# A hybrid layer on one core: feed-forward weights rounded inside the linear attention, residual and second norm by token blocks across the stage border, and value products issued later

## What is computed

```python
x = x + linear_attention(layernorm(x))     # 32 heads of 64, decayed state, rmsnorm over 2048, sigmoid gate, out_w
x = x + ffn(layernorm(x))                  # 256 -> 768 -> 256, silu(gate) * up, all three weights rounded to fp8 e4m3fn
x = x + softmax_attention(layernorm(x))    # 2 x 1024 tokens, 16 heads of 16, rotary, causal
x = x + ffn(layernorm(x))                  # the same weights and scales again

def _quantized_matmul(x, w, scale):
    wq = w.astype(jnp.float8_e4m3fn).astype(x.dtype)
    return jnp.einsum('bsi,io->bso', x, wq) * scale
```

## Time and profile before

| | us |
|---|---|
| median of 3 runs (1264.12 to 1267.35) | 1265.59 |
| the profiled execution, its own time | 1261.26 |
| its span, first to last instruction | 1259.5 |
| PE busy (14272 products) | 1116.5, 89% |
| DVE busy | 636.3, 51% |
| ACT busy | 586.5, 47% |
| POOL busy | 483.2, 38% |

### The profile page before, as it was taken

One profiled execution on the slowest core, in us unless ns is written; L12 is line 12 of the kernel. 1 busy time (PEld: TensorE's weight loads), 2 busy tenths in 40 slices (PEclk: granted clock), 3 DMA queues, 4 the chain that ended last, 5 costly groups with the idle time before them and its releaser, 6 DMA issues. The chain is left out here.

```text
span 1259.5 us, 33418 instructions
## 1 busy us (share of the span) xinstructions
PE 1116.5 (89%) x14272; PEld 866.9 (69%) x14272; DVE 636.3 (51%) x1378; ACT 586.5 (47%) x1083; POOL 483.2 (38%) x507
## 2 busy tenths in 40 slices
PE   4999999999999999999954796884899999988698
PEld 3888988988888888889843675771344444435577
DVE  6234343343343343343456736885777777743742
ACT  3544344444444443443416542341466666675442
POOL 2355354445445454453522563204122222220255
PEclk9999999999999999999975898895999999999899
DMA  3101001010010100000030002155233333000001
GB/s 117 50 2 44 9 2 51 2 44 9 2 51 3 44 8 18 35 3 2 3 116 32 1 1 84 50 150 141 49 69 68 68 69 69 19 2 1 1 17 50
DMA packets 20809, 49.01 MB, mean 39 GB/s; under 512 B 2176, under 2 KB 11968, under 8 KB 17984
## 3 DMA queue, kind: packets, MB, share of 16 engines
q1 hardware_dynamic: 20672, 46.97, 13.2%
HBM read 34.18 MB, written 8.39 MB: 34 GB/s over the span
## 5 line engine op out<-in xcount | busy, mean ns | idle before, releaser
L1514 DVE TENSOR_REDUCE ca_mx<-ca_S 128x1 f32<-128x640 f32 (+1 forms) x192 | 176.7, 955 | 64.1 <-PE ca_S L1384 63.0
L1479 ACT ACTIVATE ca_PT<-ca_ST 128x512 f32<-128x512 f32 (+1 forms) x304 | 158.3, 579 | 90.1 <-PE ca_ST L1408 88.1
L499 PE MATMUL la_R<-a_hTh,la_Wh 128*128 128x512 f32 x384 | 154.1, 401 | 3.5 <-ACT la_k L294 3.5
L423 DVE SCALAR_TENSOR_TENSOR la_y<-la_g,la_O 128x512 f32<-128x512 f32 x64 | 41.1, 684 | 228.3 <-PE la_O L587 228.3
L499 PE MATMUL la_R<-a_hTl,la_Wh 128*128 128x512 f32 x384 | 150.6, 392 | 0.0
L499 PE MATMUL la_R<-a_hTh,la_Wl 128*128 128x512 f32 x384 | 150.2, 391 | 0.0
L1355 POOL TENSOR_SCALAR_AFFINE_SELECT ca_PT<-ca_PT 128x256 f32<-128x256 f32 (+1 forms) x112 | 48.9, 442 | 204.8 <-ACT ca_PT L1479 204.6
L430 DVE TENSOR_TENSOR X<-la_R,X 128x512 f32<-128x512 f32 x64 | 44.3, 692 | 147.3 <-PE la_R L499 147.3
L241 POOL TENSOR_TENSOR la_qd<-la_q,la_C 128x512 f32<-128x512 f32 x64 | 81.3, 1291 | 96.7 <-PE la_O L587 94.6
L253 POOL TENSOR_TENSOR la_yl<-la_y,la_yh 128x512 fp32r<-128x512 f32 x64 | 81.6, 1296 | 95.4 <-ACT la_yh L318 95.4
L233 POOL TENSOR_TENSOR la_Wl<-la_Wraw,la_Wh 128x512 fp32r<-128x512 f32 (+1 forms) x32 | 50.4, 1584 | 146.4 <-DVE la_Wh L446 114.1
(11 more groups left out here) (188 smaller groups left out, 2761.2 us busy)
## 6 DMA issues: line engine op xcount, KB each, us to landing
la_Wraw<-w_quads_dram SPq DMA_DIRECT2D x7, 1280.0 KB, 5.7
ca_VG<-V SPq DMA_DIRECT2D x8, 512.0 KB, 4.8
q_parts<-rp_QP SPq DMA_DIRECT2D x4, 768.0 KB, 3.7
k_parts<-rp_KP SPq DMA_DIRECT2D x4, 768.0 KB, 3.5
ca_KS<-k_parts SPq DMA_DIRECT2D x10, 256.0 KB, 7.2
qw_w<-w_ffn_dram SPq DMA_DIRECT2D x6, 384.0 KB, 5.2
X<-hidden_dram SPq DMA_DIRECT2D x4, 512.0 KB, 7.7
la_q<-hidden_dram SPq DMA_DIRECT2D x1, 2048.0 KB, 7.6
```

The costliest lines, as they stand in the source:

```text
L499: m = pe.matmul(out, a, b, start=n == 0, stop=n == len(pairs) - 1)
L1479: act.activation(PT[:, (NM2 * g + b) % NPT, h:h + nh, 0:w], ST[at % NB][:, 0:nh * w].rearrange("p (h q) -> p h q", h=nh), ACT.Exp, scale=S ...
L1514: dve.reduce_max(out, src, AXX).then_inc(s1_free, 1)
```

## The change

**The rounding** is a class now, `quantised_weights`, with twelve chunks of 128x384 and single buffers (two of `w`). Chunk c is done by the engines inside unit 16 + c of the linear attention, units 16 to 27; SP loads each chunk and stores the rounded one to DRAM (`q_ffn`), and gathers all of it into `WF` once slot 0 of the linear attention's weights, which now lies in `WF`, is free (unit 28). The queues run passes 0 and 1 as a loop and passes 2 and 3 written out.

**The border.** The sums of squares, roots, residual and norm go by token blocks (`last_sums`, `ln2`). Blocks 0 and 1 are summed after unit 29; in unit 30 ACT takes their root and DVE adds the residual of block 0 and takes its moments; in unit 31 DVE normalises block 0 and adds the residual of block 1, and PE turns block 0. The feed-forward part begins with the sums of squares of blocks 2 and 3 and goes straight on to `up(0)`; residuals, moments, norms and turns of the later blocks stand between its steps. The residual's input is loaded by blocks; scales are loaded at its start.

**Values.** `VG` and its eight copies are gone, PE reads `V`; and four of the twelve `values` calls of a group (blocks 1, 2, 9 and 10) are issued one or two steps later. In the rotary projections `t2` has one buffer for two.

```diff
@@ linear_attention @@
-        Wh = sb("Wh", [P, 2, WTOT], F32R)
-        Wl = sb("Wl", [P, 2, WTOT], F32R)
+        Wh = [WF[:, 0:WTOT], sb("Wh", [P, WTOT], F32R)]
+        Wl = [WF[:, WTOT:2 * WTOT], sb("Wl", [P, WTOT], F32R)]
...
+            sp.wait_ge(r_ok, 2 * 4 * (NQ - 1))
+            sp.wait_ge(o_ok, 4 * (NQ - 1) + 2)
+            quant.gather(sp, 0, NQC - 2)
+            quant.store(sp, NQC - 1)
+            quant.gather(sp, NQC - 2, NQC)
+            for b in range(2):
+                sp.wait_ge(sc_ok, 4 * (NQ - 1) + b + 1)
+                sp.wait_ge(qd_ok, 2 * (4 * (NQ - 1) + b + 1))
+                sp.dma_start(q[:, b].rearrange("p a n -> p (a n)"),
+                             hidden[:, 4 * b:4 * b + 4, :].rearrange("p t n -> p (t n)")).then_inc(x_in[b], 16)
...
@@ scalar, unit @@
+                if last and j == 6:
+                    act.wait_ge(init_ok, 4)
+                    act.wait_ge(fin.ss_ok, 1)
+                    act.activation(fin.std[:, 0:8], SC[0][:, 0:8], ACT.Sqrt, bias=fin.epst[:],
+                                   scale=4.0 / FEAT).then_inc(fin.std_ok, 1)
...
                 if has(last, j, 2):
                     for pr in range(2):
                         keys(*step(i, j + 2), pr)
+                if c is not None:
+                    quant.rounding(act, c)
                 if has(last, j, 3):
                     for n in range(2):
                         evict(*step(i, j + 3), "q", n, n0 + 2 + n)
+                if c is not None:
+                    quant.overflow(act, c)
+                if last and j == 6:
+                    ln2["deviation"](act, 0)
+                if last and j == 7:
+                    ln2["high"](act, 0, banks=SC)
@@ vector, unit @@
+            def unit(i, j, last, c=None):
                 gated(i, j)
+                if last and j == 7:
+                    ln2["normalise"](dve, 0, H=hbuf)
+                    finish(1)
+                    ln2["low"](dve, 0, banks=SC)
+                    ln2["moments"](dve, 1)
                 if has(last, j, 1):
                     states(*step(i, j + 1))
+                if last and j == 6:
+                    fin.scales(dve, 0, 8, 1)
+                    finish(0)
+                    ln2["moments"](dve, 0)
                 if has(last, j, 2):
                     masks(*step(i, j + 2))
+                if c is not None:
+                    if c >= 1:
+                        quant.checked(dve, c - 1)
+                    quant.clamped(dve, c)
+                if last and j == 4:
+                    quant.checked(dve, NQC - 1)
                 for n in range(2):
                     sums(i, j, n)
+                if c is not None:
+                    quant.rounded(dve, c)
@@ tensor @@
-                if not has(last, j, 1):
-                    pe.wait_ge(sqa_ok, 8 * NQ)
-                    squares(range(0, 3 * GC))
+                if last and j == 7:
+                    pe.wait_ge(mask_ok, 8 * NQ)
+                    pe.wait_ge(fin.std_ok, 1)
+                    ln2["turn"](pe, 0, H=hbuf, banks=SC)
...
+                if u == 4 * NQ - 3:
+                    pe.wait_ge(mask_ok, 8 * NQ)
+                    pe.wait_ge(sqa_ok, 2 * (4 * NQ - 2) + 2)
+                    fin.squares(pe, range(8), SC[0])
@@ ffn, tensor @@
+                    if fin is not None and n == 3:
+                        ln["turn"](pe, 1, H=H, banks=turns)
...
+                fin.squares(pe, range(8, NT), DB[0])
             up(0)
@@ ffn, scalar @@
+                ln["deviation"](act, 1)
+                act.wait_ge(fin.ss_ok, 2)
+                act.activation(fin.std[:, 8:NT], DB[0][:, 0:8], ACT.Sqrt, bias=fin.epst[:],
+                               scale=4.0 / FEAT).then_inc(fin.std_ok, 1)
+                act.wait_ge(s_in, 32)
...
+                if fin is not None and n == 4:
+                    ln["high"](act, 1, banks=turns)
+                if fin is not None and n == 6:
+                    ln["deviation"](act, 2)
+                    ln["deviation"](act, 3)
@@ ffn, vector @@
+                if fin is not None and n in (1, 3):
+                    dve.wait_ge(x_in[2 + n // 2], 16)
+                    fin.add(dve, 2 + n // 2, H)
+                if fin is not None and n in (2, 5):
+                    ln["moments"](dve, 2 + n // 3)
+                if fin is not None and n == 4:
+                    ln["low"](dve, 1, banks=turns)
+                if fin is not None and n in (7, 9):
+                    ln["normalise"](dve, 2 + n // 9, H=H)
@@ class quantised_weights @@
+    def clamped(self, dve, c):
+        dve.wait_ge(self.w_in[c % 2], 16 * (c // 2 + 1))
+        if c >= 1:
+            dve.wait_ge(self.q_ok, c)
+        dve.tensor_scalar(self.k[:], self.w[:, c % 2], 128.0, -128.0, ALU.min, ALU.max).then_inc(self.k_ok, 1)
+
+    def rounding(self, act, c):
+        act.wait_ge(self.w_in[c % 2], 16 * (c // 2 + 1))
+        if c >= 1:
+            act.wait_ge(self.r_ok, c)
+        act.activation(self.h[:], self.w[:, c % 2], ACT.Copy, scale=0.5, saturate=False).then_inc(self.h_ok, 1)
+        act.wait_ge(self.k_ok, c + 1)
+        act.activation(self.hc[:], self.k[:], ACT.Copy, scale=0.5, saturate=False).then_inc(self.hc_ok, 1)
+        act.activation(self.e[:], self.k[:], ACT.Copy, saturate=False).then_inc(self.e_ok, 1)
@@ causal_attention @@
+        VALUES_AT = [max(LAST[b] + 3, (LAST + [NST + LAST[0]])[b + 1]) for b in range(NM2)]
...
-                    if n == LAST[0] and g >= 1:
-                        values(g - 1, NM2 - 1)
-                    for b in range(1, NM2):
-                        if n == LAST[b]:
-                            values(g, b - 1)
+                    for b in range(NM2):
+                        if VALUES_AT[b] == n + NST and g >= 1:
+                            values(g - 1, b)
+                        if VALUES_AT[b] == n:
+                            values(g, b)
```

372 lines of the change are left out of this document (182 added, 190 removed).

## The result

The kernel with the change takes 1229.23 us (median of 4 runs, 1227.77 to 1231.08), the one before 1266.47 beside it (1264.12 to 1267.67): a ratio of 0.971, interval 0.969 to 0.973, or 37 us. Measured again, as e9, it gave 0.968 (0.966 to 0.970). The profiled execution took 1230.14 us (span 1228.1). The forecast was 1223, range 1207 to 1239: the sign and the range held, the point was 6 us low. The parts fit less well: of the 36.9 us that I gave the border it brings 25 (27 in the second trace, e9), and the attention, which I gave 6, brings 11 to 12.

What follows compares the result with a forecast made beforehand. PE was taken to bound the linear attention, with PE idle at the border. Border -36.9 and attention -6 make -42.9, from 1261.26 to 1218.4 us; the 4.3 us offset to the median gives 1222.7, say 1223, range 1207 to 1239.

Steps and rivals of the forecast that it cites:

- the 36.9 us that I gave the border: From the last output products to the next stage: its end moves from 768.58 to 731.7, a gain of 36.9 us.
- Rounding inside the units, 0: Linear attention, units 16 to 27: the added rounding work costs 0 us, at most 10 us.
- The rival that the rounding chain sets the pace: Units 16 to 27: the bare rounding chain adds 60 us, giving 1283 us; chance 0.04.
- The end of the linear attention, +4.4: Units 29 to 31: sums, norm, turn and slower products make the last output products end 4.4 us later.
- the norm of block 0, taken as 2 us: Unit 31: DVE's norm of block 0 takes 2 us, between 1.38 with POOL idle and 5.52 with POOL working.
- The first feed-forward part: From its start to the next stage: 80.8 us, with 6.5 of stalls and 1.7 for a cold start.
- The check against the second feed-forward part: The second part, also starting cold, takes 76.9 us of PE; the forecast's comparable figure for the first is 78.4.
- The attention, -6 with bounds 0 and -11.4: Causal attention: later value products save half of PE's 11.4 us wait for POOL's cut; removing VG is worth 0.
- The share that I took for a wait that comes back: Causal attention: half of the 11.4 us is not gained, as an earlier PE meets DVE's maxima and ACT sooner.
- theory A of e5: Follow-up forecast at the border: moving the rounding is nearly the whole gain, dividing by blocks pays back; 1227 to 1232 us.
- the single `t2` costs nothing: Rotary projections: one buffer for t2 costs 0 us, its wait being for an older operation on the same queue.
- The norm chokes the feed-forward part: First feed-forward part: DVE and ACT extras come bare onto the path, +8 us, giving 1233 us; chance 0.15.

Runs made afterwards that it cites:

- the pair above with its allocation: Two undivided-border kernels with early residual of blocks 0 and 1: e11, 1223.61 us, and one with early moments too, many tensors moved 672 bytes in SBUF, 1229.15 us.
- e11: The undivided border of e10 with squares, root and residual of blocks 0 and 1 put early again: 1223.61 us, 0.964 of the kernel before.
- e3: The changed kernel with PE's turn of block 0 in unit 31 put behind the last output products: 1225.89 us, 0.968 of the kernel before.
- e5: The changed kernel with squares, root, residual and norm undivided, placed as in the kernel before: 1226.82 us, 0.969 of the kernel before.
- e10: The same kernel as e5, run again beside the change: 1226.28 us, 0.968 of the kernel before.
- e2: The kernel before with only the attention's change, V read directly and value products later: 1255.20 us, 0.991 of the kernel before.
- e1: The kernel before with V read directly and no VG copies, value products in their old order: 1267.73 us, 1.000 of the kernel before.

## Why the prediction was right or wrong

**Rounding inside the units, 0: right.** From 40 to 640 us PE has one wait of over 0.3 us, 0.55 at 636.25, behind the rounding (0.61 at 631.54 before), and from the `la_C` load 323 us after L0 to the one at 477 (eight units, 18 to 25, all with rounding) it takes 153.6 us, 153.4 in the kernel before. The weights' `WF` is in place before the border. The rival that the rounding chain sets the pace is gone. What the forecast lacked is that the pace of the products also moves with the kernel, by the pair above with its allocation: 0.1 us per load interval against before, under 1 us in all, but 6 us against e11.

**The end of the linear attention, +4.4: the step that failed is the norm of block 0, taken as 2 us.** It took 5.38 (5.41 in e3), nearly the 5.52 of the earlier trace rows, which I had set aside since "POOL has only `la_yl` there"; it had the squares' sums too, and each of the four tiles lasted until one of POOL's four operations had ended. On L0's clock the turn started 4.6 us later than I had put it: 3.4 from this norm, and the rest from the gate, which waited for sums behind a residual of 3.74 us, a term I had not placed in unit 30. From there on the forecast's terms held (turn 1.94 for 1.97, products 4.85 for 5.1, border 1.05 for 1.1). First `f_G`: 613.1 us after L0, forecast 652.8 - 43.8 = 609.0.

**The first feed-forward part: mis-sized by 6 to 8 us.** From the first `f_G` to the last product I had 731.7 - 2.4 - 652.8 = 76.5, measured 84.2 and 82.5. The stalls are not it: 0.20 + 2.44 + 1.80 + 1.00 (at 709.91) + 1.01 (at 727.96) are 6.5 us for my 6.5. The term that was mis-sized is the clock: 8.3 us at 0.59, 4 at 0.57 and 5 at 0.66 lose 3.4 + 1.7 + 1.7 = 6.8 us, where I had 1.7 for one cold start and nothing for the falls after each wait. The second trace of the change (e9) has no third fall and loses 4.8. And a half of `down` takes 2.88 us here and 2.72 in the earlier trace rows, up to 1.3 us over eight; I had taken a row's duration as a constant of its form. Some 1.5 us are left over in both traces. The check against the second feed-forward part should have warned me in the other direction: a part that does its whole norm at its start takes 78 us here (e5, e10, e11), and one with residual, moments, roots and norms between its steps 79.3 to 84.2. Much of that is the clock, which loses 1.6 to 2.4 us in the former and 1.6 to 6.5 in the latter, other in each execution; with this loss taken off it is 75.8 to 76.4 against 77.6 to 80.0.

**The attention, -6 with bounds 0 and -11.4: mis-sized by half.** e2 measures 12 (10 to 14 by its interval), twice my term and at its outer bound. The share that I took for a wait that comes back is what failed: it came back nowhere, and DVE's maxima, which I thought would take half of it, fell as well.

**Which part is worth what.** (Where paces are made equal below, that is worked out from the traces and was not run.) The sum of the table fell from 722.3 to 695.7 or 697.3. Moving the rounding out of the border, with nothing else at the border changed, gives 722.3 - 694.7 = 27.6, of which 5.6 is the faster pace (the squares of unit 31 start 593.0 us after L0 before and 587.4 in e10): 22.0. Dividing the border by blocks, compared at one pace (e10 plus 6.2), brings the first `f_G` 9 us earlier and costs 4 to 6 in the feed-forward part, 2.4 to 4.1 of them by the clock of these two executions: 3.6 and 5.2 us net; so theory A of e5, that it costs more than it hides, falls, although its time was met. At one pace e11 (691.4 + 6.2 = 697.6) and the change (695.7 and 697.3) are within 2 us: the lead of e11 is its pace. Less up to 1 us for the slower pace, 22.0 and these 3.6 to 5.2 give the 25 to 27 of the table. The attention brings 12. The rotary stage between, whose old trace had 82.5 us from its first turn, took 82.5 to 86.0 in the others, e1 with the old code among them 83.9 after a border 2.1 longer; behind its third turn before and after agree (64.86 and 64.87 to the attention's first DMA, 64.7 to 66.0 in the others), and over the last 64.5 us PE waits 1.46 to 1.49 us in every trace, old or new, so the single `t2` costs nothing, as forecast. Ahead of that the changed kernels lose 1.6 to 3.5 us against before and e2, in PE's waits for the first norms and in the clock; e1, with the old code, loses 3.5 as well, and why is not shown.

Of the rivals none came out whole. "The norm chokes the feed-forward part" was the nearest, by its size: 6 to 8 us, not 10, and the attention's surplus paid most of it back. Its slow operations showed (norms of 3.10 and 2.36, residuals of 3.04 and 2.71), but PE's waits were the 6.5 us of the forecast, and the excess is mostly the clock. That the point came within 6 us is two errors of opposite sign, 10 to 12 at the border and 5 to 6 in the attention, and so in part luck.
